# A fused four-layer cross-attention kernel: third attention with one set of scores, token shifts read from PSUM banks, narrow products side by side

## The reference, cut to what matters

```python
x, ctx: (64, 64, 256)                    # batch, tokens, channels
# L0: 16 heads of 16; queries from x, keys and values from [ctx, x], key mask; out_w, rmsnorm, gelu MLP, residual
# L1: RWKV block
xa = ln(x); sx = concat([state[:,1:2] - xa[:,:1], xa[:,:-1] - xa[:,1:]], 1)     # state = ctx
xxx = tanh((xa + sx*maa_x) @ maa_w1).reshape(b,l,5,32);  xxx = einsum('blfd,fde->blfe', xxx, maa_w2)
xk, xw, xv, xr, xg = xa + sx*(maa_stack + xxx)
w = exp(-exp(time_decay + tanh(xw @ td_w1) @ td_w2)); r, k, v, g = ...
step: out = r.(u*k*v + s);  s = k*v + w*s                                        # over the 64 tokens
x1 = x + groupnorm(out) * g @ Wo.T;  xc = ln(x1); sx2 = shift of xc like sx, with state[:,0:1]
x = x1 + sigmoid((xc + sx2*fmr) @ Wfr.T) * (square(relu((xc + sx2*fmk) @ Wfk.T)) @ Wfv.T)
# L2: single-head attention over ctx, residual
# L3: 32 heads of 8, 8 key heads, keys and values from ctx, mask from a (B,1,S,S) tensor
scores = q @ k.T / sqrt(8) + mask;  attn = softmax(scores);  out = attn @ v @ Wo + bo + x;  layernorm
```

## Time and profile before

| | before |
|---|---|
| median of three runs | 1704.38 us |
| profiled execution, its own time | 1702.48 us |
| profiled execution, span | 1700.6 us |
| PE busy | 1519.7 us (89%) |
| DVE busy | 1094.9 us (64%) |
| POOL busy | 680.9 us (40%) |
| ACT busy | 635.3 us (37%) |
| mean granted TensorE clock | 0.972 |

### The profile page before, as it was taken

The page is one execution under the profiler, slowest core; times in us unless marked ns, Lnnn a source line. Parts: engine busy times, 40 slices in busy tenths (PEclk is TensorE's granted clock), DMA queues, the critical chain, the costliest instruction groups (busy, mean ns, idle before and its releaser), DMA issues.

```text
span 1700.6 us, 48519 instructions
## 1 busy us (share of the span) xinstructions
PE 1519.7 (89%) x21432; PEld 1139.8 (67%) x21432; DVE 1094.9 (64%) x1829; ACT 635.3 (37%) x1325; POOL 680.9 (40%) x620
## 2 busy tenths in 40 slices
PE   5877999999999999999998999999899999997765
PEld 4655777676777767677676767777676767765544
DVE  1347576767757676775767677575867767584732
ACT  2332433533443353434334344443434344342211
POOL 1044443535243353624335452533445253343510
PEclk9889999999999999999999999999999999998977
DMA  7021121304021130403113040311304040120300
GB/s 275 9 46 21 28 54 24 66 19 74 21 46 35 23 71 13 74 20 58 24 25 70 13 74 20 67 28 17 65 18 69 20 72 22 18 42 15 50 7 8
DMA packets 74257, 73.19 MB, mean 43 GB/s; under 512 B 28480, under 2 KB 63296, under 8 KB 73664
## 3 DMA queue, kind: packets, MB, share of 16 engines
q1 hardware_dynamic: 74048, 70.09, 20.9%
HBM read 32.32 MB, written 4.19 MB: 21 GB/s over the span
## 4 chain that ended last, share of the span: by engine, by line
PE 58%; DVE 23%; POOL 11%; issue 5%; ACT 2%; DMA 1%; DVEq 0%; POOLq 0%; SPq 0%; ACTq 0%
PE pw L395 21%; PE pw L373 8%; PE pw L595 7%; PE pw L379 5%; PE pw L589 5%; DVE mx L1068 5%; POOL ab L1027 4%; DVE ab L1211 4%; POOL ab L993 2%; DVE tB L1107 2%; PE pw L703 2%; PE pw L502 1%; DVE ptC L1258 1%; POOL c L1046 1%; DVE tC L1107 1%
## 5 line engine op out<-in xcount | busy, mean ns | idle before, releaser
L1211 DVE TENSOR_TENSOR_SCAN ab<-wS,ab 128x260 f32<-128x260 f32 x256 | 276.6, 1135 | 19.5 <-ACT ab L913 16.7
L1027 POOL TENSOR_TENSOR ab<-ab,kvrg 128x512 f32<-128x512 f32 x128 | 165.7, 1294 | 92.7 <-DVE ab L1211 92.7
L993 POOL TENSOR_TENSOR ab<-big,kvrg 128x512 f32<-128x512 f32 x128 | 184.9, 1449 | 6.0 <-DMA big<-kvrg 5.8
L1068 DVE TENSOR_REDUCE mx<-pw 128x16 f32<-128x1024 f32 (+1 forms) x128 | 149.3, 1205 | 27.5 <-PE pw L395 27.5
L1016 POOL TENSOR_TENSOR big<-big,xaB 128x512 f32<-128x512 f32 x80 | 95.4, 1207 | 171.6 <-DVE big L1190 171.6
L373 PE MATMUL pw<-big,wb 128*128 128x256 f32 x512 | 128.6, 395 | 0.5 <-issue 0.5
L589 PE MATMUL pw<-tA,wb 128*128 128x256 f32 x512 | 127.1, 398 | 0.7 <-DVE tA L1161 0.7
L595 PE MATMUL pw<-wb,ptA 128*128 128x256 f32 x512 | 119.4, 387 | 0.0
L978 POOL TENSOR_TENSOR vtmp_A<-mv_A,eps 128x2 f32<-128x2 f32 x16 | 3.1, 195 | 289.7 <-DVE mv_A L1088 289.7
L589 PEld LDWEIGHTS pw<-tA,wb 128*128 128x128 f32 x512 | 96.4, 195 | 28.6 <-issue 15.6
L373 PEld LDWEIGHTS pw<-big,wb 128*128 128x128 f32 x512 | 94.0, 193 | 24.4 <-issue 12.8
(11 more groups left out here) (212 smaller groups left out, 3210.7 us busy)
## 6 DMA issues: line engine op xcount, KB each, us to landing
big<-kvrg SPq DMA_DIRECT2D x256, 128.0 KB, 3.8
hT<-in_h SPq DMA_DIRECT2D x16, 512.0 KB, 5.7
wb<-in_wb SPq DMA_DIRECT2D x1, 5056.0 KB, 23.4
a<-in_x SPq DMA_DIRECT2D x16, 256.0 KB, 4.3
xB<-in_x SPq DMA_DIRECT2D x16, 256.0 KB, 2.9
m<-in_amask SPq DMA_DIRECT2D x64, 64.0 KB, 2.1
result<-c SPq DMA_DIRECT2D x16, 256.0 KB, 2.0
m<-in_mask SPq DMA_DIRECT2D x16, 128.0 KB, 2.6
```

Source lines behind the costliest of these rows:

```text
L993: G.tensor_tensor(ab[i % 4][:, :, :, 1:S + 1], vx[i % 3].rearrange("p j (b s) -> p j b s", b=NB), k, ALU.mult).then_inc(a_ok, 1)
L1027: G.tensor_tensor(ab[i % 4][:, :, :, 0:S], st[i % 2][:, :, :, 0:S], r, ALU.mult).then_inc(pd_ok, 1)
L1068: V.tensor_reduce(mx[:, 2 * j:2 * j + 2, g * p:g * p + g], pw[:, 2 * j:2 * j + 2, :].rearrange("p r (g s) -> p r g s", g=g), AXX, ALU.max) ...
L1211: last = V.tensor_tensor_scan(st[i % 2][:, j, :, :].rearrange("p b s -> p (b s)"), wS[:, i // 4, :, :].rearrange("p b s -> p (b s)"), ab[i ...
```

## The change: what it does

Third attention. The second set of scores, the transposed mask and the subtraction by product are gone. `max1` computes the scores as before; DVE takes the maxima and then subtracts them, reading each bank and writing `ms` in SBUF (new, four instructions per half). ACT takes the exponential in SBUF (now stage `turn1`, twice). PE turns the exponentials into the banks with 32 transpositions per tile (stage `exp1`), and ACT copies them into `pt`. `max1` 1 now waits until the subtraction of the first half is done.

Token shifts. DVE reads the shifted value straight from the bank. The first token of each sequence comes from a small table `first`, made once from the two context rows (`e0`, a new load). `xaC`, its POOL difference and the combining instructions are gone. ACT squares `fk`. Both banks of `cturn` are now read to the end by DVE.

Narrow products. The 32-row block of `mix1` is computed as four products of 64 tokens in four column groups, and `pw1` as two of 128 tokens in two column groups; ACT reads them with four and two instructions.

The order string has one stage more (83 letters) and is another one throughout.

```diff
-ORDER = "AABAACBABCCBACACCBBABCBAACBAACABBCBBBBBCCBBCABCBBCBABBCAACBBBBCABBBBCBBACCABACCCBB"
+ORDER = "AABACBABBCCCBBABCCBACBBCBBBCBBBBBBACCABBCAACBABBCABABBABCAABAABBCCBBBACACCCCBCCBACB"
...
-                elif name == "exp1" and i == 1 and t + 1 < TILES:
-                    sp.wait_ge(e_ps, 2 * TURN[1, t] + 2)
+                elif name == "turn1" and i == 1 and t + 1 < TILES:
+                    sp.wait_ge(a_ps, 2 * TURN[1, t] + 2)
                     load_mask(t + 1)
...
 # PE, mix1
+                    for k in range(2):
+                        for b in range(NB):
+                            last = into(b5[group(b), 0:S], w("m1", k)[:, P:P + 32], tB[:, k, b * S:(b + 1) * S], k == 0, k == 1)
...
 # PE, pw1
-                        last = mm(kn(b5)[0:64, 0, :], w("td1", k), xm[1][:, k, :], start=(k == 0), stop=(k == 1))
+                        for c in range(TT):
+                            last = into(b5[64 * c:64 * c + 64, 0:P], w("td1", k), xm[1][:, k, tok(c)], k == 0, k == 1)
...
 # PE, max1 (second half), turn1, exp1
-                        pe.wait_ge(a_mx, 4 * a + 2)
+                        pe.wait_ge(su_ok, t * 4 + 2)
                     max_scores(1, i)
-                elif name == "turn1":
-                    pe.wait_ge(a_mx, 4 * TURN[1, t] + 4)
-                    nc.tensor.transpose(ps[0][:, 0:P], mx[:, :, :].rearrange("p r j -> p (r j)"), ident).then_inc(mt_ps, 1)
                 elif name == "exp1":
-                    if i == 0:
-                        pe.wait_ge(mt_sb, TURN[1, t] + 1)
-                    else:
-                        pe.wait_ge(e_sb, 4 * TURN[1, t] + 2)
-                    exp_scores(1, i)
+                    for j in range(2):
+                        pe.wait_ge(ex_ok, t * 4 + 2 * i + j + 1)
+                        if i == 0:
+                            pe.wait_ge(su_ok, t * 4 + 2 + j + 1)
+                        else:
+                            pe.wait_ge(e_sb, 4 * TURN[1, t] + j + 1)
+                        for r in (2 * j, 2 * j + 1):
+                            for c in range(4):
+                                last = nc.tensor.transpose(ps[r][:, tok(c)], ms[:, i, r, tok(c)], ident)
+                        last.then_inc(ex_ps, 1)
...
 # ACT, fk, turn1, exp1
+                    A(flat(kkS), flat(fkS), ACT.Square).then_inc(kk_ok, 1)
...
+                    for j in range(2):
+                        act.wait_ge(su_ok, t * 4 + 2 * i + j + 1)
+                        A(ms[:, i, 2 * j:2 * j + 2, :], ms[:, i, 2 * j:2 * j + 2, :], ACT.Exp).then_inc(ex_ok, 1)
                 elif name == "exp1":
-                    weights(1, TURN[1, t], i)
+                    for j in range(2):
+                        act.wait_ge(ex_ps, t * 4 + 2 * i + j + 1)
+                        A(pt[1][i][:, 2 * j:2 * j + 2, :], pw[:, 2 * j:2 * j + 2, :], ACT.Copy).then_inc(e_sb, 1)
...
 # POOL, cturn
-                    shift(sxC.rearrange("p k (b s) -> p k b s", b=NB), xaC, sxC_ok)
...
 # DVE, token shifts
+            def mixed(to, m, k, src):
+                v = seqs(to[:, k, :])[:, :, 1:S]
+                return V.scalar_tensor_tensor(v, seqs(src)[:, :, 0:S - 1], aff[:, m, 2, k:k + 1], v, ALU.mult, ALU.add)
+            def mixed_first(to, m, t):
+                v = to.rearrange("p k (b s) -> p k b s", b=NB)[:, :, :, 0]
+                return V.tensor_tensor(v, v, first[:, m, :, t * NB:(t + 1) * NB], ALU.add)
...
 # DVE, cturn
-                    shifted(xaC, tC, 1, kn(bank(k + 1))[:, 1, :], "ln2w", "ln2b").then_inc(read(k + 1)[0], 2)
-                    mixed(xaC, tC, "fmk").then_inc(ff_d, 1)
-                elif name == "fk":
-                        last = V.scalar_tensor_tensor(seqs(thC[:, k, :]), seqs(sxC[:, k, :]), vec("fmr", k), xaC[:, k, :, 1:S + 1], ALU.mult, ALU.add)
-                elif name == "l2k":
-                    V.tensor_tensor(kkS, fkS, fkS, ALU.mult).then_inc(kk_ok, 1)
+                    affine(tC, 1, kn(bank(k + 1))[:, 1, :], "ln2b").then_inc(ct_d, 1)
+                    affine(thC, 2, kn(bank(k + 1))[:, 1, :], "ln2b").then_inc(ct_d, 1)
+                    mixed(tC, 1, 1, kn(bank(k + 1))[:, 1, :])
+                    mixed_first(tC, 1, t)
+                    mixed(tC, 1, 0, kn(bank(k))[:, 0, :]).then_inc(ff_d, 1)
+                    mixed(thC, 2, 1, kn(bank(k + 1))[:, 1, :]).then_inc(read(k + 1)[0], 2)
+                    mixed_first(thC, 2, t).then_inc(ff_d, 1)
+                    mixed(thC, 2, 0, kn(bank(k))[:, 0, :]).then_inc(read(k)[0], 2)
...
 # DVE, max1
                     maxima(1, TURN[1, t], i)
+                    for j in range(2):
+                        dve.wait_ge(a_mx, 4 * TURN[1, t] + 2 * i + j + 1)
+                        for r in (2 * j, 2 * j + 1):
+                            last = V.tensor_tensor(ms[:, i, r, :].rearrange("p (g s) -> p g s", g=8), ps[r].rearrange("p (g s) -> p g s", g=8),
+                                                    mx[:, r, 8 * i:8 * i + 8].unsqueeze(2).broadcast_to([P, 8, S]), ALU.subtract)
+                        last.then_inc(su_ok, 1)
```

More of the change, by code:

```diff
@@ L49, in attention @@
 def attention(layer):
-    return [(f"{name}{layer}", p) for name, ps in (("max", 2), ("turn", 1), ("exp", 2), ("value", 2), ("out", 2)) for p in range(ps)]
+    return [(f"{name}{layer}", p) for name, ps in (("max", 2), ("turn", 1 + layer), ("exp", 2), ("value", 2), ("out", 2)) for p in range(ps)]
 def scans():
@@ L165, in build @@
         eps = sb("eps", [P, 4])
-        aff = sb("aff", [P, 2, 3, 2])
+        aff = sb("aff", [P, 3, 4, 2])
+        e0 = sb("e0", [P, 2, KT, B])
+        first = sb("first", [P, 3, KT, B])
         power = sb("power", [P, TT])
@@ L442, in exp_scores @@
+                            into(ps[r][:, (2 * i + j) * P:(2 * i + j + 1) * P], kT[group(r), j, 2 * p + i, :], qz[group(r), j, 2 * p + i, :, :],
+                                 i + j == 0, False)
                 for i in range(2):
-                    b = 2 * p + i
                     for j in range(2):
                         for r in range(4):
-                            out = ps[r][:, (2 * i + j) * P:(2 * i + j + 1) * P]
-                            if layer == 0:
-                                at = 4 * p + 2 * i + j
-                                last = into(out, w("pick")[group(r), at:at + 1].broadcast_to([32, P]), mT[group(r), :], False, i + j == 2)
-                            else:
-                                for e in range(2):
-                                    at = 4 * b + 2 * j + e
-                                    last = into(out[e * S:(e + 1) * S, :], w("pick")[group(r), at:at + 1].broadcast_to([32, S]),
-                                                mT[group(r), :], False, i + j == 2)
+                            at = 4 * p + 2 * i + j
@@ L455, in exp_scores @@
+                            last = into(ps[r][:, (2 * i + j) * P:(2 * i + j + 1) * P], w("pick")[group(r), at:at + 1].broadcast_to([32, P]),
+                                        mT[group(r), :], False, i + j == 2)
                 last.then_inc(e_ps, 1)
@@ L609, in part_b @@
                     pe.wait_ge(xin_ok, t + 1)
-                    for m in range(2):
-                        wide = P if m == 0 else 32
-                        for k in range(2):
-                            last = mm(kn((b4, b5)[m])[0:wide, m, :], w("m1", k)[:, m * P:m * P + wide], tB[:, k, :], start=(k == 0), stop=(k == 1))
-                        last.then_inc(m1_ps, 1)
+                    for k in range(2):
+                        last = mm(kn(b4)[:, 1, :], w("m1", k)[:, 0:P], tB[:, k, :], start=(k == 0), stop=(k == 1))
+                    last.then_inc(m1_ps, 1)
+                    for k in range(2):
+                        for b in range(NB):
+                            last = into(b5[group(b), 0:S], w("m1", k)[:, P:P + 32], tB[:, k, b * S:(b + 1) * S], k == 0, k == 1)
+                    last.then_inc(m1_ps, 1)
                 elif name == "mix2":
@@ L825, in part_a @@
                     act.wait_ge(*full(k))
+                if t == 0 and name == "norm0":
+                    fold_first()
                 if name == "q0":
                     if t:
-                        act.wait_ge(e_ps, 2 * TURN[0, t - 1] + 2)
+                        act.wait_ge(e_ps, 2 * t)
                     for c in range(2):
@@ L887, in part_b @@
                     act.wait_ge(pk_ps, t * 6 + 3)
-                    A(thB[0:64, 0, :], kn(b5)[0:64, 0, :], ACT.Tanh).then_inc(pk_sb, 1)
+                    for c in range(TT):
+                        last = A(thB[0:64, 0, c * P:(c + 1) * P], b5[64 * c:64 * c + 64, 0:P], ACT.Tanh)
+                    last.then_inc(pk_sb, 1)
                 elif name == "pr":
@@ L928, in part_c @@
                 if name == "cturn":
-                    A(xaC[:, :, :, 0:1], hT[t % 3][:, :, :, 0:1], ACT.Copy)
-                    shifted(xaC, tC, 1, kn(bank(k))[:, 0, :], "ln2w", "ln2b").then_inc(read(k)[0], 2)
```

(5 more changed lines are left out.)

133 lines of the change are left out of this document (60 added, 73 removed).

## The result

The changed kernel takes 1716.58 us (median of five runs, 1713.57 to 1719.3), the kernel before 1703.74 in the same series (1700.34 to 1704.4). The ratio is 1.0083, with an interval of 1.0064 to 1.0102.

A forecast was written before the change was run, and what follows sets the result against it. PE was taken to bound most of it. Iteration 97.0 against 98.40 us, fifteen giving -21, head and tail -4: span 1700.6 to 1675.6, plus 1.9 and 1.9, 1679 us; 8-in-10 range 1630 to 1722.

The forecast's parts named there:

- PE's work: PE's busy time per iteration: 4.8 us less, from 92.6 to 87.8 us.
- PE's idle time: Summed waits of PE in one new iteration, mostly in the scan: 9.2 us instead of 6.
- the walk: One iteration of the new order followed with timeline durations, looking for each wait of PE; 9.2 us idle.
- the wait before `oturn`: In the scan, PE done at about 18.3 us, first half of `oturn` at about 20.7: PE waits 2.4 us.
- rival 3: Third attention: transpositions do not overlap in long runs, 5.7 us more per tile, 1765 us; 0.05, shared with another new wait.
- 87.8 + 9.2 = 97.0: One steady iteration: PE's busy plus idle time gives 97.0 us against 98.40, so -1.4 us.
- After that `max1` 0 and the four `up` cover the last steps: Scan stretch, behind `zturn`: this PE work covers the last scan steps on DVE, so no further wait is counted there.
- Rival 2: Gap before `zturn`: the granted clock falls, 1.2 to 3.3 us lost per tile, 1715 us given; chance 0.29.
- fifteen iterations give -21 us: Whole kernel: the gain of 1.4 us per iteration counted fifteen times.
- without that cover it would be 5.1 us: Third attention: `max1` 1 waits for maxima and subtractions, costing nothing behind about 8 us of `up` and `sum`, otherwise 5.1.
- The edges proper: Head and tail: shorter shifts and the tail's third attention without second scores save 4 us.
- issue gaps: Inside the removed PE groups: if these go too, PE's saving per tile is 4.8 us rather than 4.5.

The follow-up runs named there:

- experiment 2: The changed kernel with the first `max1` issued on PE ahead of the first `oturn` instead of after `zturn`; 1709.15 us, ratio 1.0047 to the kernel before.
- experiment 1: The changed kernel with idle products on PE in the three gaps before the first `oturn`, the third `sum` and `zturn`; 1689.78 us, ratio 0.993 to the kernel before.
- Experiment 9: The kernel before with only the narrow products side by side; 1710.35 us, ratio 1.0053.
- experiments 8: The kernel before with only the new token shifts, the square on ACT and the narrow products, old third attention and order; 1680.07 us, ratio 0.9854.

## Why the prediction was wrong

**What held.** PE's work: experiment 2 has the same 1066 instructions in an iteration at full clock, and there PE is busy 88.1 us, forecast 87.8 (it is 89.65 in the changed kernel, at a clock of 0.98). PE's idle time: the waits of one iteration sum to 9.2 to 9.5 us, forecast 9.2, and the largest stand where the walk put them, 1.27 before `oturn` (forecast 2.4), 1.54 before `sum` (1.0), 1.65 before `zturn` (1.4). That the sum agrees is in part luck: the wait before `oturn` was to be 2 to 3 us. The walk's own terms up to `oturn` (0.7, four steps of 2.27, 0.7, 0.9, 0.7, 4.4 and two steps of 1.7) add up to 19.9 us and not to 20.7, which would have put the wait at 1.6. The 32 transpositions take 3.9 us, forecast 3.5, start to start 0.12 us; rival 3 is out. The narrow products take 0.44 and 0.66 us per tile (7.1 and 10.5 us in 16; forecast 0.3 and 0.55). Subtractions take 681 ns (692) and DVE 70.0 us (70). `up` and `down` cover them in the steady part. With the clock held (experiment 1) the iteration is 97.5 us, forecast 97.0. The Trainium skill's figure for one transposition (TensorE: Matmul & The Clock Gate, Part 4: PE-mode transpose), about 275 ns, given there with bf16, is near the length of 288 ns that these float32 ones have, and again not near the price in a run.

**The step that failed first** is the sum "87.8 + 9.2 = 97.0", which puts the fall of the clock at nothing, with the words "After that `max1` 0 and the four `up` cover the last steps". They cover them, but `zturn` and `max1` 0 come out of the gaps slowly: 1.09 us for `zturn` and 2.09 for the sixteen score products, against 0.63 and 1.15 in experiment 1 (`up` has the full clock again here; in experiment 2 it is the one that is slow). The walk itself had found PE working about 1 us of 5.8 before `zturn`, and the earlier trace rows had the clock at 0.50 to 0.70 in or just behind stretches with 2.4 to 2.6 us of work in 4. The changed kernel's rows are of that kind: 2.40 and 1.14 of 4, then 0.65. Rival 2 was then the consequence of my own forecast, not an alternative to it; its 0.29 was far too low. The loss lies in its range of 1.2 to 3.3 us, near the low end: 1.6 us per iteration, 22 us over fourteen. That the result is also near the 1715 of rival 2 is luck: by the rival's own sum 1.6 us lost per iteration give about 1703, and the rest came from the next point and from idle time.

**The second** is "fifteen iterations give -21 us". The fifteenth has no part A. The prediction wrote of the subtractions that "without that cover it would be 5.1 us" and did not ask which iteration is without it. It lost 10.4 us, where -1.4 was counted. The runs show more in it than the subtractions, which PE waits for 3.7 us: its wait for the scan's product grew from 4.0 to 10.5 us, and 5.1 of the 10.4 us are busy time at the lower clock. The edges proper (-4 forecast) came out at -6.8.

**The balance against the forecast.** Span, measured +16.1 against -25.0: 41.1 us. Fourteen full iterations: 32.1, of which the clock is 22, the 0.5 us by which the thirteen steady ones exceed 97.0 even in experiment 1 are 7, and the first one, which takes 3.7 us more than 97.0 there, is the rest. The iteration without part A: 11.8. Edges: -2.8.

**A premise that the forecast did not state** is that work taken off PE is time. It gave the narrow products 1.3 us and the attention 3.2 per tile on that ground (and 0.3 for issue gaps, a term that no run shows: the busy time fell by 4.5 us at full clock, not 4.8). Experiment 9 took 0.9 us off PE for nothing. In the change itself the idle time grew as the work shrank, 5.8 to 9.2 us: I forecast both numbers rightly and still read PE as the bound. A chain through part B that PE waits for would do that, and the shorter shifts lie on it; that the chain is the cause is argued from experiments 8 and 9, and no run isolates one link of it.

**What stays open.** Why the narrow products alone make the kernel 0.5% slower was not tried. Nor do the runs tell what part of the 1.7 us per iteration is each of the three shifts, or the square that went to ACT, or how much of the changed kernel's waits in the iteration without part A a held clock would take away.

## What to carry to other kernels

When a change opens gaps on TensorE, add up the gaps first and read what the clock did after gaps like them elsewhere in the same trace; if it fell there, the fall belongs in the forecast, and idle products in the wait are a cheap test (here -27 us). Count iterations by what they hold: a wait that a neighbouring stage covers is open wherever that stage has run out. When two parts of a change were made for each other, setting back one of them tells little about its share (here either alone left 27 us of idle time). Before freed work on the busiest engine is counted as time, ask whether that engine waits for a chain; here the edit that shortened instructions on the other engine (the shifts, 25 us) was worth more than the one that freed the busiest (nothing).
